# A macaron block with chunked delta-rule attention: 32x32 triangular inverses made as two 16x16 inverses and a join on TensorE

## What is computed

```python
x = x + 0.5 * ffn(layernorm(x))          # 256 -> 1024 -> 256, gelu
x = x + attn(layernorm(x))
x = x + 0.5 * ffn(layernorm(x))
...
A = -jnp.tril(jnp.einsum('bhncd,bhned->bhnce', kb, k), -1)
T = solve_triangular(eye - A, jnp.broadcast_to(eye, A.shape), lower=True)
u = T @ v
w = T @ kb
```

## Time and profile before

| | us |
|---|---|
| median of three runs | 1430.82 (1430.59 to 1433.77) |
| the profiled execution | 1438.96 |
| span of its trace | 1437.3 |
| PE busy | 1162.0 |
| VectorE busy | 837.3 |
| ScalarE busy | 503.4 |
| GpSimd busy | 390.5 |

### The profile page before, as it was taken

How to read it: one execution, slowest core, us unless ns; L and a number is a source line. 1 busy time by engine, 2 the same in 40 slices (tenths; PEclk the granted TensorE clock), 3 DMA queues, 4 the chain that set the end, 5 groups by cost and what they waited for, 6 DMA issues and landing times.

```text
span 1437.3 us, 27174 instructions
## 1 busy us (share of the span) xinstructions
PE 1162.0 (81%) x10172; PEld 836.3 (58%) x10172; DVE 837.3 (58%) x1534; ACT 503.4 (35%) x809; POOL 390.5 (27%) x597
## 2 busy tenths in 40 slices
PE   4766688889878988789887998689887898788847
PEld 3633574378535875378634785268743785367626
DVE  5752266665666556565666657664666657644354
ACT  2142135323343335323353324423353234531222
POOL 6008200750018300560008400380007500281000
PEclk9888798889989999889988999889999899877678
DMA  4040103110040201210030200401030100401000
GB/s 131 16 88 1 29 16 69 21 29 17 15 89 1 45 16 46 43 29 18 15 89 0 45 1 16 89 16 31 16 71 18 29 16 1 88 1 43 1 0 16
DMA packets 80265, 47.47 MB, mean 33 GB/s; under 512 B 55808, under 2 KB 73728, under 8 KB 80128
## 3 DMA queue, kind: packets, MB, share of 16 engines
q1 hardware_dynamic: 80128, 45.56, 13.9%
HBM read 30.86 MB, written 14.68 MB: 32 GB/s over the span
## 4 chain that ended last, share of the span: by engine, by line
PE 50%; DVE 29%; issue 8%; ACT 6%; SPq 3%; POOL 2%; DMA 1%; DVEq 1%; ACTq 0%; POOLq 0%
PE psum L730 10%; PE psum L731 9%; PE psum L732 9%; DVE conv_acc L1276 7%; PE psum L761 3%; DVE h_lo L1256 3%; DVE arena L1501 3%; PE psum L1021 2%; PE psum L911 2%; PE psum L900 2%; DVE arena L1233 2%; SPq L336 2%; PE psum L1090 1%; DVE bn L1221 1%; DVE arena L1503 1%
## 5 line engine op out<-in xcount | busy, mean ns | idle before, releaser
L505 POOL TENSOR_TENSOR l_prod<-arena 64x30 f32<-64x30 f32 (+14 forms) x240 | 142.9, 595 | 776.3 <-DMA arena<-l_dram 758.1
L558 ACT ACTIVATE h_f<-psum,b_col 128x512 f32<-128x512 f32 x128 | 88.1, 689 | 291.7 <-PE psum L732 227.8
L730 PE MATMUL psum<-w_hi,h_hi 128*128 128x256 f32 x512 | 154.7, 302 | 32.3 <-DVE h_lo L1256 32.3
L1021 PE MATMUL psum<-v_shift,fir_w 128*32 128x512 f32 x1152 | 144.1, 659 | 10.7 <-DMA v_shift<-v_dram 10.6
L509 POOL TENSOR_TENSOR arena<-arena,l_prod 64x30 f32<-64x30 f32 (+14 forms) x240 | 145.3, 605 | 18.8
L732 PE MATMUL psum<-w_hi,h_lo 128*128 128x256 f32 x512 | 147.7, 288 | 0.0
L731 PE MATMUL psum<-w_lo,h_hi 128*128 128x256 f32 x512 | 147.4, 288 | 0.0
L730 PE MATMUL psum<-xt_hi,w_hi 128*128 128x512 f32 x256 | 120.0, 469 | 32.2 <-DVE xt_lo L1242 14.0
L1256 DVE TENSOR_TENSOR h_lo<-h_f,h_hi 128x512 fp32r<-128x512 f32 x128 | 129.8, 1014 | 4.4
L1255 DVE CAST h_hi<-h_f 128x512 fp32r<-128x512 f32 x128 | 69.5, 543 | 103.5 <-ACT h_f L558 51.4
L1276 DVE SCALAR_TENSOR_TENSOR conv_acc<-psum,conv_col,conv_acc 128x511 f32<-128x511 f32 x144 | 107.8, 748 | 36.8 <-ACT conv_acc L583 18.4
(11 more groups left out here) (221 smaller groups left out, 2255.1 us busy)
## 6 DMA issues: line engine op xcount, KB each, us to landing
x_in<-in_L_attn_x SPq DMA_DIRECT2D x8, 512.0 KB, 3.4
v_dram<-v_fm SPq DMA_DIRECT2D x8, 512.0 KB, 2.8
v_shift<-v_dram SPq DMA_DIRECT2D x8, 512.0 KB, 5.0
out<-x_tok SPq DMA_DIRECT2D x8, 512.0 KB, 4.4
v_shift<-v_dram SPq DMA_DIRECT2D x8, 511.0 KB, 7.1
v_shift<-v_dram SPq DMA_DIRECT2D x8, 510.0 KB, 9.0
v_shift<-v_dram SPq DMA_DIRECT2D x8, 509.0 KB, 11.7
arena<-in_L_ffn_w SPq DMA_DIRECT2D x2, 1024.0 KB, 7.1
```

The source lines that it names most:

```text
L505: pool.tensor_tensor(prod, l_inv[:, k + 1:, k:k + 1].broadcast_to(shape), l_inv[:, k:k + 1, 0:k].broadcast_to(shape), ALU.mult).then_inc(i ...
L558: act.activation(h_f[:, m % 2, :], bank, ACT.Gelu, bias=b1_col[:, m:m + 1]).then_inc(read, 1)
L730: pe.matmul(dst, a_hi, b_hi, start=first, stop=False, **kw)
L1021: last = pe.matmul(banks[p][0][col:col + 32, :], fir_w[:, group, n, :], v_shift[:, group, at_t:at_t + T], start=(n in (0, TAPG)), stop=(n ...
```

## The change

Each 32x32 matrix is L = [[A, 0], [B, C]] with 16x16 blocks. POOL now inverts the diagonal blocks A and C alone, 128 matrices of 16x16 on all 128 partitions: 14 pairs of instructions in place of 30, the largest with 56 elements in place of 240. PE joins them: `block_y` multiplies B (`l_block`, `l_tok` with a mask, a new POOL instruction) with the inverse of A, ACT copies the result to `y_block`, and `block_x` makes the lower left block of the inverse and of its transpose, which ACT puts into `x_t` and `t_low` (one copy, then four and three). In a pass with a back, `block_y` stands before step 10 of the second feed-forward block and `block_x` before step 14. In the head no such block exists, and both stand between "lhalf" and "lpair". The wait for the loads moves from `merge` to the start of `block_y`. The loads become 8 + 8 + 14 DMAs of half the row length (4 + 4 + 6 before); `l_turned` and `l_prod` move into the unused part of the arena slot of `l_inv`; the clearing of `t_low` covers all of it. The four row groups of one product write four partition quarters of one PSUM bank.

```diff
-        L_OFF = [("lhalf", (5, 6)), ("lpair", (5, 6))]
+        L_OFF = [("lhalf", (5, 6)), ("yb", (5,)), ("xb", (6,)), ("tb", (0,)), ("lpair", (5, 6))]
...
-                    for c in range(CPT):
-                        sp.dma_start(l_inv[UNITS * c:UNITS * c + UNITS, :, :],
-                                     l_dram[c].rearrange("i u j -> u i j")).then_inc(l_loaded, 16)
+                    for e in range(BPT):
+                        col = BLOCK * (e % 2)
+                        sp.dma_start(l_inv[UNITS * e:UNITS * e + UNITS, :, :],
+                                     l_dram[e, :, :, col:col + BLOCK].rearrange("i u j -> u i j")).then_inc(l_loaded, 16)
...
+                    for e in range(BPT):
+                        rows = slice(BLOCK * e, BLOCK * e + BLOCK)
+                        sp.dma_start(x_t[rows, :, rows], tt_dram[e].rearrange("u j i -> j u i")).then_inc(t_loaded, 16)
+                    sp.wait_ge(t_zeroed, j + 1)
+                    for e in range(BPT - 1):
+                        col = CHUNK * (e // 2 % 2) * (e < 6) + BLOCK * (e % 2)
                         for g in range(2):
...
+                    pool.wait_ge(l_made, j + 1)
+                    pool.sem_inc(passed, 1)
+                    pool.tensor_tensor(l_block[:, :, :], l_tok[:, :, :],
+                                       low_block[:, :].unsqueeze(1).broadcast_to([P, UNITS, CHUNK]), ALU.mult).then_inc(l_masked, 1)
+                    pool.wait_ge(l_loaded, 16 * BPT * (j + 1))
                     n = 0
-                    for k in range(1, CHUNK - 1):
-                        below = CHUNK - 1 - k
-                        shape = [CPT * UNITS, below, k]
+                    for k in range(1, BLOCK - 1):
+                        below = BLOCK - 1 - k
+                        shape = [P, below, k]
...
+                if at.front:
+                    out_of(at, "yb", 0, y_block[:, :, BLOCK:], src=lambda b: pairs(b)[:, :, BLOCK:])
+                if at.back:
+                    gelu(at, 1, i, 4)
...
-                pe.wait_ge(t_loaded, 16 * T_LOADS * i + 16 * T_LOADS)
...
+            def block_y(at):
+
+                pe.wait_ge(t_loaded, 16 * T_LOADS * (at.j + 1))
+                pe.wait_ge(l_masked, at.j + 1)
+                bank, full = claim(pe, at, "yb")
+                pe.sem_inc(passed, 1)
+                for u in range(UNITS):
+                    for c in range(CPT):
+                        rows = slice(32 * c, 32 * c + 32)
+                        last = pe.matmul(bank[rows, 32 * u:32 * u + 32], l_block[rows, u, :], x_t[rows, u, rows],
+                                         start=True, stop=True)
+                last.then_inc(full, 1)
+
+            def block_x(at):
+                copied(pe, at, "yb")
+                bank, full = claim(pe, at, "xb")
...
+                        last = pe.matmul(bank[rows, 32 * u:32 * u + 32], t_low[rows, u // 8, u % 8, col:col + CHUNK],
+                                         y_block[rows, u, :], start=True, stop=True)
...
-                pair_at, next_at = 18, len(STEPS) - 4
+                y_at, x_at, pair_at, next_at = 10, 14, 18, len(STEPS) - 4
```

More of the change, by code:

```diff
@@ L20 @@
 CPT = P // CHUNK
+BLOCK = 16
+BPT = P // BLOCK
 UNITS = TILES * HEADS
@@ L50, in macaron_kernel @@
         low_strict = sb("low_strict", [P, CHUNK])
+        low_block = sb("low_block", [P, CHUNK])
         up_incl = sb("up_incl", [P, P])
@@ L524, in one_pass @@
                     pool.sem_inc(passed, 1)
-                    pool.memset(t_low[0:CHUNK, :, :, CHUNK:D], 0.0).then_inc(c1v_made, 1)
+                    pool.memset(t_low, 0.0).then_inc(t_zeroed, 1)
                     copied(pool, at, "v_t", 1)
@@ L717, in one_pass @@
                     high(at, 2, i, "ln3")
-                    for m in range(KT):
+                    for m in range(4):
+                        gelu(at, 1, i, m)
+                if at.front:
+                    out_of(at, "yb", 0, y_block[:, :, BLOCK:], src=lambda b: pairs(b)[:, :, BLOCK:])
+                if at.back:
+                    gelu(at, 1, i, 4)
+                if at.front:
+                    for c in range(CPT):
+                        rows = slice(32 * c, 32 * c + BLOCK)
+                        bank, x_read = arrive(act, at, "xb")
+                        x_last = act.activation(x_t[rows, :, 32 * c + BLOCK:32 * c + CHUNK], pairs(bank[rows, :])[:, :, BLOCK:], ACT.Copy)
+                    x_last.then_inc(x_read, 1)
+                    for c in range(CPT - 1):
+                        rows, col = slice(32 * c, 32 * c + 32), CHUNK * (c % 2)
+                        bank, t_read = arrive(act, at, "tb")
+                        t_last = act.activation(t_low[rows, :, :, col:col + BLOCK],
+                                                bank[rows, :].rearrange("p (g u j) -> p g u j", g=2, j=CHUNK)[:, :, :, 0:BLOCK],
+                                                ACT.Copy)
+                    t_last.then_inc(t_read, 1)
+                if at.back:
+                    for m in range(5, KT):
                         gelu(at, 1, i, m)
@@ L1007, in off_diagonal @@
                                 last.then_inc(banks[p][1], 1)
+            def block_y(at):
[4 more added lines that the diff above has]
+                for u in range(UNITS):
+                    for c in range(CPT):
+                        rows = slice(32 * c, 32 * c + 32)
+                        last = pe.matmul(bank[rows, 32 * u:32 * u + 32], l_block[rows, u, :], x_t[rows, u, rows],
[4 more added lines that the diff above has]
+                bank, full = claim(pe, at, "xb")
+                pe.sem_inc(passed, 1)
+                for u in range(UNITS):
+                    for c in range(CPT):
+                        rows, col = slice(32 * c, 32 * c + 32), CHUNK * (c % 2) * (c < 3)
+                        last = pe.matmul(bank[rows, 32 * u:32 * u + 32], t_low[rows, u // 8, u % 8, col:col + CHUNK],
+                                         y_block[rows, u, :], start=True, stop=True)
+                last.then_inc(full, 1)
+                bank, full = claim(pe, at, "tb")
+                pe.sem_inc(passed, 1)
+                for u in range(UNITS):
+                    for c in range(CPT - 1):
+                        rows, col = slice(32 * c, 32 * c + 32), CHUNK * (c % 2)
+                        last = pe.matmul(bank[rows, 32 * u:32 * u + 32], y_block[rows, u, :],
+                                         t_low[rows, u // 8, u % 8, col:col + CHUNK], start=True, stop=True)
+                last.then_inc(full, 1)
             def firs(at, a, between=None):
@@ L1123, in one_pass @@
                     off_diagonal(at, "lhalf")
-                pair_at, next_at = 18, len(STEPS) - 4
+                y_at, x_at, pair_at, next_at = 10, 14, 18, len(STEPS) - 4
                 if at.back:
                     turn_rows(at, "ln3", xn_made[2], i + 1)
-                    for n in range(pair_at):
+                    for n in range(y_at):
+                        ffn_step(at, 1, i, n)
+                if at.front:
+                    block_y(at)
+                if at.back:
+                    for n in range(y_at, x_at):
+                        ffn_step(at, 1, i, n)
+                if at.front:
+                    block_x(at)
+                if at.back:
+                    for n in range(x_at, pair_at):
                         ffn_step(at, 1, i, n)
```

52 lines of the change are left out of this document (28 added, 24 removed).

## The result

The changed kernel took 1504.12 us (median of 4 executions, 1493.11 to 1510.12) against 1432.30 for the kernel before in the same rounds: a ratio of 1.049, with a 95% interval from 1.042 to 1.056. The forecast was 1427.6, with a range from 1414 to 1448. The profiled execution took 1498.76 us, with a span of 1497.0 us against 1437.3.

What follows compares the result with a forecast made beforehand. PE, busy 81% of the span, was taken as the bound, with gains where it waits for or is disturbed by GpSimd. -5 + 12.3 - 7.5 - 3 = -3.2 us, applied to the 1430.82 median: 1427.6 us, range 1414 to 1448.

Steps and rivals of the forecast that it cites:

- Added on PE: ... 352 records: Pass with a back: 352 joining records at 12 ns add 4.2 us, bounds 2.8 and 13 us.
- The head, -5 us: Before the loop: shorter inversion starts the first merge earlier; -5 us, bounds -9 and +1.
- The bank wait: Pass, before step 10: `block_y` waits for bank 5, which VectorE reads in "lhalf"; 0.65 us.
- rival 4: Join's loads arrive late in each pass; a 2 us wait gives +14, 1441.6 us; chance 0.05.
- The layer norm: Before the second feed-forward block: without GpSimd beside it, it shrinks by 1.3 us a pass.
- The stalls for `h_lo`: Second feed-forward block: GpSimd no longer meets `split` 3, so the stall goes; -1.8 us a pass on average.
- +12.3 - 7.5 - 3 = +1.8: Seven passes: +12.3 us net from join and waits, -7.5 and -3 from less half-clock time.
- The clock, -10.5 us: Passes: five half-clock stretches after the stall go, -7.5 us; those opening the block shrink, -3, bounds 0 and -10.
- Rival 2: Join costs 19 ns a record and half-clock stretches stay: +22, 1452.6 us; chance 0.22, including a half of it.
- Rival 3: Join's four row groups run one after another at 37 ns a record: +79, about 1510 us; chance 0.06.

Runs made afterwards that it cites:

- e11: Changed kernel with third joining product and `lpair` each four steps later, plus 32 TensorE instructions once in the head: 1443.69 us, ratio 1.010.
- e1: Changed kernel with each of the three joining products made for one of its 16 units only: 1420.21 us, ratio 0.991.
- e5: Changed kernel with 64 more TensorE instructions a pass ahead of the grams, third joining product and `lpair` four steps later: 1461.31 us, ratio 1.023.
- e7: Kernel before the change with its four `v_shift` loads a pass cut from 512 to 64 columns: 1459.78 us, ratio 1.025.

## Why the prediction was wrong

**The step that failed** is the first of the pass: "Added on PE: ... 352 records", priced at 12 ns each, 4.2 us, with "Nothing is queued behind but PE's own steps" beside it. The price of a record was if anything too high (8.5 ns at full clock). What had no term is that each record is an instruction, and its weight load another, and that these have to be brought. Rows of before with 128 records show the pace of products already fetched, 256 instructions of them; the join has 448 in a row in a pass and 704 in the head. The profile had shown the supply: the q8 line of the page, and "issue" 8% of the chain, which I read as a constant. Measured: 14.7 us of waits in `tb`, 24.8 in the grams, and the half clock behind both; clearing both (e11) took the time from 1504 to 1444.

**The head, -5 us.** GpSimd's part was right: done at 121.58 (forecast 122.3), the wait before `block_y` over at 136.67 (139.0). The join behind it was not:

```profile
136.67 1.93 PE L1058 MATMUL psum<-x_t,l_block 32*32 32x32 f32 x128 [9.27 <-DMA v_shift<-t_dram]
...
141.36 0.52 PE L1069 MATMUL psum<-y_block,v_shift 32*32 32x32 f32 x36 [0.83 <-issue]
...
145.35 0.32 PE L1077 MATMUL psum<-v_shift,y_block 32*32 32x32 f32 x5 [2.47 <-issue]
```

It took 8.9 us, not 4.7, and the first merge starts at 156.55 instead of 153.7, as in the kernel before (156.65). With the join cut (e1) it starts at 150.24; with the whole join and the full loads the earliest is e5's 154.38, so no run reached the forecast. e11 says nothing on this: its traced execution was already 7 us behind at the head's grams, ahead of the join.

**A pass.** The bank wait: 0.67 us, forecast 0.65. The loads land in time, so rival 4 is out. The layer norm takes 1.38 us as forecast, and "lhalf" to the block is 1.1 us a pass shorter (forecast 1.3). The stalls for `h_lo` in the second block, 12.4 us before, are gone in all seven. For the join's own price e11 is the test, since its passes have the join without the waits (the two that are left are in its head): from the block to the next merge 253.2 us against 239.6, from "lhalf" to the block 38.4 against 46.2, together +5.8. That includes what the clock gives back in these stretches, so it stands beside +12.3 - 7.5 - 3 = +1.8 of the forecast. Against e1, which has the bank wait too and spends as long at half clock there, e11 takes 26.8 us more from the block to the merge (226.4 in e1): 3.8 a pass for the products that I priced at 4.2. So the price of the products held, a little on the high side; what failed is that they would be there in time.

**The clock, -10.5 us**: in the changed kernel the waits in `tb` bring back half-clock stretches (PEclk 0.54 above), and its mean is 0.874 against 0.886. In e11 it is 0.891. From the block to the next merge, PE spends 57.7 us of the seven passes at half clock before, 58.9 in the changed kernel and 32.3 in e11. The gain was real but needs the join free of pauses.

**The rivals.** Rival 2 came nearest in kind and was right that a half-clock stretch can follow the joins, but gave the wrong reason and 22 us instead of 72. Rival 3 named nearly the right time, 1510, and that was luck: four row groups writing one bank run at 8.5 ns a record, not 37. The Trainium skill's rule behind it ("TensorEngine Tiling (Array Packing)", "Gotcha 1: PSUM Pressure") shows no cost here, where the groups write different partitions of the bank. The Trainium skill's floor of about 25 ns between starts ("TensorE: Matmul & The Clock Gate", "Wait — 56ns, not 53.3ns?") does not hold for these products either: 8.5 ns.

## What to carry to other kernels

Count the instructions that an edit adds, not only their busy time: here TensorE gets 256 every 3 to 4 us, and tiny ones that it uses up at 256 in 1.08 us outrun that. Look at the instruction queue of the profile, and ask which bulk transfers run where a fetch comes due. When a change slows lines that it does not touch, pad the code ahead of them by a fraction of a fetch and by a whole one, before explaining it by what the change does: here 64 instructions in the head moved the time by 41 us and 256 by no more than the noise.

## What the runs showed of the hardware that was not expected

- TensorE's program comes in transfers of 16.4 KB on a DMA queue of its own, and one that comes due beside 2 MB of loads starts 5 to 6 us later than with an eighth of their bytes (6.5 to 7.4 us after the first gram product instead of 0.9 to 2.5). PE stood still for 8.2 us instead of 2.2.
- The time depends on where a loop lies in the program: 1460.6 us with a shift of 64 instructions, 1501.6 with 256, 1504.1 with none.
- Small products that go round four tiles of the array ran 8.5 ns apart at full clock, with the four row groups in one PSUM bank.
- A product of GpSimd on 64x130 elements that takes 0.44 us in the head of the kernel before takes 2.38 in e7 beside VectorE's 2048-column ones; VectorE's went from 4.62 to 4.81 us.
